# Local attention's projection: the keys split on GpSimd, both norms' weights on the keys, turned keys copied by VectorE too

## The reference

```python
q = (x @ wq + bq).reshape(B, T, H, D).transpose(0, 2, 1, 3)
k = (x @ wk + bk).reshape(B, T, H, D).transpose(0, 2, 1, 3)
q = _rmsnorm(q, qn_w)        # t * rsqrt(mean(t * t) + eps) * w, over the 8 columns of a head
k = _rmsnorm(k, kn_w)
scores = jnp.einsum('bhqd,bhkd->bhqk', q, k) / jnp.sqrt(jnp.float32(D))
```

## Time and profile before

| | |
|---|---|
| median of 3 runs | 1747.12 us (1745.82 to 1751.17) |
| profiled execution | 1757.22 us, its span 1755.9 us |
| mean granted clock of TensorE | 0.834 of full speed |
| busy over the whole span | PE 71%, DVE 68%, ACT 54%, POOL 32% |
| this stage, from the first bias to the last row copy | about 123.85 to 197.96 us |

### The profile page before, as it was taken

One profiled execution on the slowest core, in us unless ns is written; L12 is line 12 of the kernel. 1 busy time (PEld: TensorE's weight loads), 2 busy tenths in 40 slices (PEclk: granted clock), 3 DMA queues, 4 the chain that ended last, 5 costly groups with the idle time before them and its releaser, 6 DMA issues. The chain is left out here.

```text
span 1755.9 us, 36353 instructions
## 1 busy us (share of the span) xinstructions
PE 1238.1 (71%) x13313; PEld 624.7 (36%) x13313; DVE 1196.7 (68%) x3279; ACT 947.0 (54%) x1500; POOL 570.0 (32%) x1032
## 2 busy tenths in 40 slices
PE   2754564366757788899886464776778898988746
PEld 2653453365532122222232453353222222223246
DVE  4358598436777899987862354277789999786234
ACT  0226774122445688888875240134557788887522
POOL 2331276146662411321123242275332111112323
PEclk9977675577577999999998695856799999999869
DMA  9410000021001100000000180000000000000012
GB/s 243 102 46 1 1 4 2 22 66 50 1 18 53 35 1 1 1 2 3 1 1 13 49 217 27 2 1 1 1 1 2 1 2 1 1 2 1 13 44 81
DMA packets 59137, 49.01 MB, mean 28 GB/s; under 512 B 7105, under 2 KB 54194, under 8 KB 58610
## 3 DMA queue, kind: packets, MB, share of 16 engines
q1 hardware_dynamic: 53282, 35.84, 7.9%
q0 software_dynamic: 4736, 9.74, 1.7%
q10 hardware_dynamic: 944, 1.10, 0.2%
HBM read 32.72 MB, written 18.38 MB: 29 GB/s over the span
## 5 line engine op out<-in xcount | busy, mean ns | idle before, releaser
L1709 ACT ACTIVATE arena<-psum 128x1024 f32<-128x1024 f32 (+3 forms) x640 | 561.0, 898 | 191.6 <-PE psum L1602 170.8
L1761 DVE TENSOR_REDUCE arena<-psum 128x1 f32<-128x512 f32 x768 | 479.8, 683 | 63.4 <-PE psum L1592 59.7
L1618 PE MATMUL psum<-arena 128*9 128x256 f32 (+2 forms) x4352 | 346.4, 394 | 0.9 <-POOL arena L1826 0.4
L1592 PE MATMUL psum<-arena 64*128 64x512 bf16 (+3 forms) x1280 | 240.2, 371 | 128.7 <-DVE arena L1761 58.3
L1766 DVE CUSTOM_DVE_ANT_0 arena<-psum,wqkv 128x384 bf16<-128x384 f32 (+3 forms) x512 | 230.3, 486 | 89.0 <-PE psum L1592 75.1
L1602 PE MATMUL psum<-arena 64*128 64x512 bf16 (+3 forms) x1280 | 233.7, 362 | 20.0 <-ACT arena L1709 15.0
L1826 POOL TENSOR_SCALAR_AFFINE_SELECT arena<-arena 128x256 f32<-128x256 f32 x256 | 103.6, 408 | 323.0 <-ACT arena L1709 320.4
L1592 PEld LDWEIGHTS psum<-arena 64*128 64x128 bf16 x1280 | 64.0, 94 | 383.2 <-DVE arena L1761 196.6
L1618 PEld LDWEIGHTS psum<-arena 128*9 128x9 f32 x4352 | 67.7, 89 | 174.3 <-issue 133.5
L1804 POOL CAST arena<-arena 128x16 bf16<-128x16 f32 x64 | 16.4, 257 | 327.7 <-DVE arena L1772 325.4
L677 DVE TENSOR_SCALAR small<-psum,YT 128x128 f32<-128x128 f32 x168 | 50.5, 342 | 78.0 <-PE psum L587 77.4
(11 more groups left out here) (353 smaller groups left out, 1962.9 us busy)
## 6 DMA issues: line engine op xcount, KB each, us to landing
arena<-taps SPq DMA_DIRECT2D x8, 1024.0 KB
big_w<-in_w SPq DMA_DIRECT2D x2, 2048.0 KB
ACCn<-made_rows SPq DMA_DIRECT2D x16, 256.0 KB, 3.6
regions<-sorted_rows SPq DMA_DIRECT2D x5, 741.8 KB, 4.6
sorted_rows<-arena SPq DMA_DIRECT2D x2, 1483.5 KB, 16.8
ACCn<-regions SPq DMA_DIRECT2D x32, 64.5 KB, 1.9
w<-in_w SPq DMA_DIRECT2D x2, 1024.0 KB
ACCn<-sorted_rows SPq DMA_DIRECT2D x6, 258.0 KB, 3.4
```

The source lines that it names most:

```text
L1592: pe.matmul(psum[:, b, 0:w], plain_q[v % 2][rows, a, i * P:(i + 1) * P], keys[rows, 2 * hq + a, c * GW:c * GW + w], start=True, stop=True) ...
L1618: mm = pe.matmul(psum[32 * hh:32 * hh + 9, O_BANK, lo:hi], values[:, tile_of(v, j), 4 * hq + hh, :], prob[(t + hh // 2) % N_PROB][:, hh % ...
L1709: act.activation(prob[t % N_PROB][:, :, off:GW], both, ACT.Exp, scale=INV_SQRT_HD).then_inc(a_got, 1)
L1761: dve.tensor_reduce(place, bank[:, 0:w], AX.X, ALU.max).then_inc(a_max_got, 1)
```

## The change

POOL multiplies the keys' weight by the queries' weight once, on 8 columns, and then the keys by both; DVE's multiplication of the queries goes. POOL splits the keys (three casts, two subtractions, a remainder `rest_k` of its own), DVE the queries alone. Of the turned rows DVE copies keys 5 and 7 of each group and in the last group all four keys; ACT copies the others. PE waits for the parts and copies of queries before the query rows, and for those of keys before the key rows. ACT makes the copies of key parts behind the row copies 0 and 1. DVE's biases wait, from group 2 on, until POOL no longer reads the `raws` buffer that they fill.

```diff
@@ names
-            rest = take(105 * K, GT * D).rearrange("p (n d) -> p n d", d=HD)
+            rest, rest_k = (take(k * K, GT * D).rearrange("p (n d) -> p n d", d=HD) for k in (105, 109))
@@ GpSimd
+            def copied_by_dve(r):
+
+                return r % 8 in (5, 7) or r >= 8 * NG - GT
+
+            def wait_rows_copied(e, r):
+
+                e.wait_ge(w_rows_dve if copied_by_dve(r) else w_rows_act,
+                          sum(copied_by_dve(r_) == copied_by_dve(r) for r_ in range(r + 1)))
...
+                own_pool(pool.tensor_tensor(qk_w[:, 1, :], qk_w[:, 1, :], qk_w[:, 0, :], ALU.mult))
+                pool.wait_ge(w_k_part, 1)
                 for g in range(NG):
                     rows = heads(raws[g % 2][:, 1, :, :])
                     pool.wait_ge(w_scaled, g + 1)
-                    pool.tensor_tensor(rows, rows, qk_w[:, 1, :].unsqueeze(1).broadcast_to([P, GT * NH, HD]), ALU.mult).then_inc(w_weighed, 1)
+                    own_pool(pool.tensor_tensor(rows, rows, qk_w[:, 1, :].unsqueeze(1).broadcast_to([P, GT * NH, HD]), ALU.mult))
+                    if g:
+                        pool.wait_ge(w_rows_turned, 8 * g)
+                    src = rows
+                    for m in range(3):
+                        pool.tensor_copy(part_of(split_k, K_PARTS[m][0]), src).then_inc(w_k_part, 1)
+                        pool.wait_ge(w_k_part, 3 * g + m + 2)
+                        if m < 2:
+                            own_pool(pool.tensor_tensor(rest_k, src, part_of(split_k, K_PARTS[m][0]), ALU.subtract))
+                            src = rest_k
@@ TensorE
                 def to_slots(g):
-                    pe.wait_ge(w_part, 6 * g + 6)
-                    pe.wait_ge(w_copied, 6 * g + 6)
                     for k, src in enumerate((split_q, split_k)):
+                        pe.wait_ge(w_k_part if k else w_q_part, 3 * g + 3 + k)
+                        pe.wait_ge(w_copied, 6 * g + 3 + 3 * k)
...
                             if r >= 2:
-                                pe.wait_ge(w_rows, r - 1)
+                                wait_rows_copied(pe, r - 2)
@@ ScalarE
+                def turned(g, tiles):
+                    for r in (8 * g + t for t in tiles):
+                        if not copied_by_dve(r):
+                            act.wait_ge(w_rows_turned, r + 1)
+                            act.activation(rows_to(r), turned_rows(r), ACT.Copy).then_inc(w_rows_act, 1)
+
                 for k in range(NG + 4):
                     if 0 <= k - 4:
-                        split_copies(k - 4)
+                        split_copies(k - 4, 0)
...
                     if 0 <= k - 4:
-                        for r in range(8 * (k - 4), 8 * (k - 4) + 8):
...
+                        turned(k - 4, (0, 1))
+                        split_copies(k - 4, 1)
+                        turned(k - 4, (2, 3, 4, 6))
@@ VectorE
                 def biased(g):
...
+                    if g >= 2:
+                        dve.wait_ge(w_k_part, 3 * (g - 2) + 3)
...
-                    rows = heads(raws[g % 2][:, 0, :, :])
-                    chain(dve.tensor_tensor(rows, rows, qk_w[:, 0, :].unsqueeze(1).broadcast_to([P, GT * NH, HD]), ALU.mult))
 
                 def split(g):
-                    for k, (dst, parts) in enumerate(((split_q, Q_PARTS), (split_k, K_PARTS))):
...
+                    src = heads(raws[g % 2][:, 0, :, :])
+                    if g:
+                        dve.wait_ge(w_rows_turned, 8 * (g - 1) + 4)
+                    for m in range(3):
+                        dve.tensor_copy(part_of(split_q, Q_PARTS[m][0]), src).then_inc(w_q_part, 1)
...
+                def turned(g):
+                    for r in range(8 * g, 8 * g + 8):
+                        if copied_by_dve(r):
+                            dve.wait_ge(w_rows_turned, r + 1)
+                            dve.tensor_copy(rows_to(r), turned_rows(r)).then_inc(w_rows_dve, 1)
...
                         ln_statistics(n, k)
+                    if 0 <= k - 4:
+                        turned(k - 4)
```

More of the change, by code:

```diff
@@ L725, in build @@
         w_turned, w_yt, w_projected, w_raw, w_squared = (sem(n) for n in ("w_turned", "w_yt", "w_projected", "w_raw", "w_squared"))
-        w_mean, w_root, w_scaled, w_weighed, w_part, w_copied, w_rows_turned, w_rows = (
-            sem(n) for n in ("w_mean", "w_root", "w_scaled", "w_weighed", "w_part", "w_copied", "w_rows_turned", "w_rows"))
-        w_bias_in, w_padded = sem("w_bias_in"), sem("w_padded")
+        w_mean, w_root, w_scaled, w_q_part, w_k_part, w_copied, w_rows_turned, w_rows_act, w_rows_dve = (
+            sem(n) for n in ("w_mean", "w_root", "w_scaled", "w_q_part", "w_k_part", "w_copied", "w_rows_turned", "w_rows_act", "w_rows_dve"))
+        w_bias_in = sem("w_bias_in")
         s_set_up, s_first, s_values, s_kept, s_cut, s_fourfold, f_spread = (
@@ L757, in project_pool @@
                 pool.memset(split_q[:, :, 48:64], 0.0)
-                pool.memset(split_k[:, :, 48:64], 0.0).then_inc(w_padded, 1)
+                pool.memset(split_k[:, :, 48:64], 0.0).then_inc(w_k_part, 1)
                 pool.wait_ge(const_in, CONST_IN)
+                own_pool(pool.tensor_tensor(qk_w[:, 1, :], qk_w[:, 1, :], qk_w[:, 0, :], ALU.mult))
+                pool.wait_ge(w_k_part, 1)
                 for g in range(NG):
@@ L762, in project_pool, with rows_to, turned_rows @@
                     pool.wait_ge(w_scaled, g + 1)
-                    pool.tensor_tensor(rows, rows, qk_w[:, 1, :].unsqueeze(1).broadcast_to([P, GT * NH, HD]), ALU.mult).then_inc(w_weighed, 1)
+                    own_pool(pool.tensor_tensor(rows, rows, qk_w[:, 1, :].unsqueeze(1).broadcast_to([P, GT * NH, HD]), ALU.mult))
[8 more added lines that the diff above has]
+                            src = rest_k
+            def rows_to(r):
+                base = r // 8 * GW + (r % GT) * P
+                return keys[:, :, W + base:W + base + P] if r % 8 >= GT else queries[:, :, base:base + P]
+            def turned_rows(r):
+                return psum[:, 4 + r % 2, :].bitcast(BF16).rearrange("p (a t) -> p a t", a=8)
             def project_pe():
@@ L805, in project_act, with split_copies @@
             def project_act():
-                def split_copies(g):
-                    for k, (dst, parts) in enumerate(((split_q, Q_PARTS), (split_k, K_PARTS))):
[L808 to L813, removed]
+                def split_copies(g, k):
+                    dst, parts = ((split_q, Q_PARTS), (split_k, K_PARTS))[k]
+                    if g:
+                        act.wait_ge(w_rows_turned, 8 * (g - 1) + 4 + 4 * k)
+                    for m in range(2):
+                        act.wait_ge(w_k_part if k else w_q_part, 3 * g + m + 1 + k)
+                        for other in parts[m][1:]:
+                            act.activation(part_of(dst, other), part_of(dst, parts[m][0]), ACT.Copy).then_inc(w_copied, 1)
+                def turned(g, tiles):
[3 more added lines that the diff above has]
+                            act.activation(rows_to(r), turned_rows(r), ACT.Copy).then_inc(w_rows_act, 1)
                 for k in range(NG + 4):
                     if 0 <= k - 4:
-                        split_copies(k - 4)
+                        split_copies(k - 4, 0)
                     if 0 <= k - 3 < NG:
@@ L858, in head_normed @@
                     dve.wait_ge(w_scaled, g + 1)
-                    rows = heads(raws[g % 2][:, 0, :, :])
-                    chain(dve.tensor_tensor(rows, rows, qk_w[:, 0, :].unsqueeze(1).broadcast_to([P, GT * NH, HD]), ALU.mult))
                 def split(g):
[L863 to L875, removed]
+                    dve.wait_ge(w_k_part, 1)
+                    src = heads(raws[g % 2][:, 0, :, :])
+                    if g:
+                        dve.wait_ge(w_rows_turned, 8 * (g - 1) + 4)
+                    for m in range(3):
+                        dve.tensor_copy(part_of(split_q, Q_PARTS[m][0]), src).then_inc(w_q_part, 1)
+                        dve.wait_ge(w_q_part, 3 * g + m + 1)
+                        if m < 2:
+                            chain(dve.tensor_tensor(rest, src, part_of(split_q, Q_PARTS[m][0]), ALU.subtract))
+                            src = rest
+                def turned(g):
[3 more added lines that the diff above has]
+                            dve.tensor_copy(rows_to(r), turned_rows(r)).then_inc(w_rows_dve, 1)
                 dve.wait_ge(const_in, CONST_IN)
```

## The result

The changed kernel takes 1764.23 us, the median of 4 runs (1760.79 to 1765.29); the kernel before, run beside it, 1747.39 (1745.82 to 1751.17). The ratio is 1.009, interval 1.0068 to 1.0112: slower by 16.8 us. The forecast was 1763.5.

A forecast was written before the change was run, and what follows sets the result against it. DVE sets the pace first, ACT later, with DVE a group ahead; chained passes of 23.2 + 19.8 + 17.8 + 14.6 = 75.4 against 58.95 add 16.4 to 1747.12, giving 1763.5 us, range 1753.5 to 1773.

The forecast's parts named there:

- group 0: First pass between scaling ends: split, sums to YT copy, row copies, row chain, scaling in one chain, 23.2 us.
- the stage: Local attention from its layer norm to line 898's barrier; forecast to grow from 58.95 to 75.4 us between marks.
- the first mark: End of DVE's first scaling by the norms' roots, where the forecast's intervals start; expected at about 139 us.
- The split in turns, S: DVE's queries' split alternating with GpSimd's work on the keys at their shared port, 5.2 us per group.
- The waits: DVE idle 7 to 9 us ahead of its row copies in the first three groups, released by PE's turns.
- Groups 1 and 2: Second and third passes between scaling ends, the same chain with PE rows at 0.65: 19.8 and 17.8 us.
- Tail: Last group to the stage's end, DVE copying its four key rows: 14.6 us, 3.8 less than before.
- The sum: Three groups and the last stretch together: 75.4 us against 58.95, so 16.4 us longer.
- The anchor: Difference put on the timed median 1747.12, not the profiled execution 10.1 us above it; new profiled execution expected at 1773.6.
- no turns at the port: Rival: DVE's casts and subtractions run at full pace beside GpSimd's, split 2.8 us; 1753.9 us, chance 0.11.
- GpSimd dearer: Rival: GpSimd's instructions cost more, split 7.7 us, each group 2.5 longer; 1773.5 us, chance 0.11.
- DVE never waits: Rival: key row 7 is turned in time, DVE alone sets the pace, 9.8 us shorter; 1737.3 us, chance 0.05.

The follow-up runs named there:

- e1_late: Changed kernel with DVE's row copies of each group moved behind the next group's split of the queries: 1751.25 us, ratio 0.9967 to the kernel before.
- e3_noport: Changed kernel with GpSimd neither weighing nor splitting the keys, which stay zero, small memsets giving the signals: 1763.12 us, ratio 1.0038 to the kernel before.
- e2_none: Changed kernel with ACT making all row copies and none on DVE, keys still split on GpSimd: 1756.2 us, ratio 0.9993 to the kernel before.

## Why the prediction was right

The time (1763.5 forecast, 1764.23 measured) and its mechanism stood. That the time was hit to 0.7 us is in part luck: errors of -0.5 us in group 0 and +2.1 in the rest of the stage, 0.5 at the first mark and 1.5 between the stage's end and 930 us partly cancel. Step by step:

- *The split in turns, S.* Forecast 5.2; measured 138.48 to 142.96 + 0.72 = 143.68, 5.20. Two of its parts were off in opposite ways: a GpSimd subtraction alone takes 1.16 (e1_late), not the 1.05 of the earlier trace rows, and the waiting GpSimd instruction hides 0.15 of itself under DVE's end (its cast ended 0.46 behind DVE's, 141.08 against 140.62, where it takes 0.61 alone). The cast is the 0.61 that was extrapolated. The Trainium skill, "GPSIMD Engine Reference", section 3.1 "Elementwise — side-by-side cycle accounting", gives estimates of 1.11 and 0.77 for the two: the runs agree on the first, where it was nearer than the row taken, and not on the second.
- *The waits.* Forecast: DVE idle 7 to 9 us ahead of line 909, released by line 821, in three groups. Measured 8.15, 7.43 and 6.68, the third a little under the range (and 6.79 in the tail). e3_noport keeps all four without GpSimd's work; e1_late brings the first three to 1 us or less by place alone.
- *Group 0.* Forecast 23.2, measured 22.67. Its part from the end of the copy to YT (149.87) to the end of DVE's second copy (159.03) was 9.16 where 9.9 were forecast, in part because row 4 came at 0.61 and not at the 0.95 taken; the part from S to that copy was 6.2 instead of 5.9.
- *Groups 1 and 2.* Forecast 19.8 and 17.8, measured 20.66 and 18.50. The mis-sized term is PE's row: 0.65 was taken, the rows came at 0.95 (1.89 for two). The prediction had that case in its range as "3 more"; these two groups and the tail together came out 2.1 longer. Line 884 adds 0.25 in each of groups 0 to 2: 0.48 beside GpSimd's last cast, 0.23 without it (e1_late from group 1 on).
- *Tail.* Forecast 14.6, measured 15.11, and before 18.42. Here the division of the copies pays, as said.
- *The sum.* Forecast 75.4, measured 76.94; the first mark came 0.5 earlier, so the stage ends 17.5 later, and 16.0 of that is still there at 930 us.
- *The anchor.* The 10.1 us between before's profiled execution and its median were put on the new one's, which would have made it 1773.6; it took 1763.24. The difference belonged to that one execution, so starting from the median was right and the figure for the new profiled execution wrong.

Of the rivals, "no turns at the port" falls by the 0.72 and 1.5 to 1.6 rows, "GpSimd dearer" by S, and "DVE never waits" by the three idles. e1_late shows that the last named a real possibility with the wrong condition: not a fast enough row 7, but copies that stand behind the next split; what it gains there is 2.7 us of stage, not the 9.8 of that rival. The Trainium skill, "Perfetto Trace Analysis", section "Optimizing Scalar/DVE Operations", warns that moving work between DVE and GpSimd might not help, because of their shared port. e2_none agrees (58.98 against 58.95), though for another reason: ACT was the pace.

## What to carry to other kernels

When an engine that runs ahead takes over the last step of a pipeline, look at what stands behind that step in its queue: it will wait for the whole chain of the group before it starts the next one. Put the step behind the next group's first work that others wait for. Here that alone turned a loss of 0.9% into a gain of 0.3%, each against the kernel before on its own chip.

## What had not been expected of the hardware

Of two instructions that take turns, the later one ends less than its own length behind the other: DVE's cast 0.29 behind (0.43 alone), GpSimd's cast 0.46 behind (0.61 alone). A copy of a turned row from PSUM on DVE takes 0.69 where it stands alone, 0.68 in the earlier trace rows. In e1_late one of them, 158.38 to 159.07, ran beside a GpSimd cast, 158.48 to 159.09, and neither was longer than alone (0.69 and 0.61): these two did not take turns.

PE's slow rows lasted: in the last three stretches of the changed kernel its granted clock was near the lower level (0.55 to 0.58 of full speed), and a row took 0.95 instead of 0.61. It is tempting to put that on the idles of 5 to 8 us that the loop leaves it. The runs do not show it. In e1_late, where DVE runs ahead again, the rows came as slow:

```profile
167.99 1.86 PE L821 MATMUL psum<-identb,arena 128*128 128x128 bf16 x16 [1.94 <-ACT arena L847]
164.57:176.97 12.40, 7.79 (x73) 6.49 (x74) 7.84 (x12) 10.16 (x15) 5.81 (x6) 0.58 0.01 1
```

The idles in that stretch are under 2 us, and its clock is 0.58 all the same; the third stretch of the kernel before had 0.63. What made the clock fall here stays open.
